# A graph-attention layer on one core: the order of the first 25 microseconds and of the last instructions

## The reference

```python
h = jnp.maximum(_layernorm(x, axis=-1), 0.0)
# the attention layer on h
h = node_features @ W.T + b_W
e = (h @ a1)[:, None] + (h @ a2)[None, :] + b_a[0]
e = jnp.where(e > 0, e, 0.2 * e)
scores = jnp.where(adjacency_matrix > 0, e, jnp.float32(NEG_INF))
attention = jax.nn.softmax(scores, axis=1)
h_prime = attention @ h
# and last
x = x + h_prime
```

## Time and profile before

| | |
|---|---|
| device time, median of 3 | 209.23 us (208.92 to 209.34) |
| the profiled execution | 209.82 us, its span 208.2 us |
| PE busy | 198.0 us, 95% of the span |
| DVE busy | 183.3 us, 88% |
| ACT busy | 141.4 us, 68% |
| POOL busy | 47.5 us, 23% |
| DMA | 75.66 MB, mean 363 GB/s |

### The profile page before, as it was taken

How to read it: one execution, slowest core, us unless ns; L and a number is a source line. 1 busy time by engine, 2 the same in 40 slices (tenths; PEclk the granted TensorE clock), 3 DMA queues, 4 the chain that set the end, 5 groups by cost and what they waited for, 6 DMA issues and landing times.

```text
span 208.2 us, 7164 instructions
## 1 busy us (share of the span) xinstructions
PE 198.0 (95%) x3176; PEld 191.8 (92%) x3176; DVE 183.3 (88%) x268; ACT 141.4 (68%) x129; POOL 47.5 (23%) x65
## 2 busy tenths in 40 slices
PE   0998999999999999999999999999999999999993
PEld 0686789899999999999999999999999999999992
DVE  3828997999999999987999998979998899989753
ACT  2388866997671777779775766798677737987000
POOL 1052879899950020440000000000000000000000
PEclk9999999999999999999999999999999999999999
DMA  5999999999999999999999999999999999980321
GB/s 180 352 416 406 404 402 410 404 404 404 413 422 405 409 408 408 405 411 408 406 407 408 390 391 416 409 407 408 410 407 406 378 416 409 411 336 37 104 66 40
DMA packets 24160, 75.66 MB, mean 363 GB/s; under 512 B 1600, under 2 KB 5952, under 8 KB 24000
## 3 DMA queue, kind: packets, MB, share of 16 engines
q1 hardware_dynamic: 23984, 75.06, 91.7%
q10 hardware_dynamic: 144, 0.13, 0.3%
HBM read 73.08 MB, written 2.11 MB: 361 GB/s over the span
## 4 chain that ended last, share of the span: by engine, by line
issue 60%; DMA 14%; PE 12%; ACT 5%; DVE 4%; POOL 3%; SPq 1%; POOLq 0%
DMA adj_sb<-in_adj_t 12%; ACT mask L380 5%; PE ps L752 3%; PE ps L762 3%; DMA wp<-in_w_pack 2%; DVE w L452 2%; PE ps L784 1%; PE ps L786 1%; PE ps L790 1%; SPq L313 1%; POOL tx L733 1%; POOL bad L738 1%; POOL tt L735 1%; POOL bad L737 1%; DVE stats L523 1%
## 5 line engine op out<-in xcount | busy, mean ns | idle before, releaser
L784 PE MATMUL ps<-V,w 128*128 128x129 f16 x1024 | 177.3, 219 | 0.7 <-DVE V L566 0.3
L786 PE MATMUL ps<-V,w 128*128 128x129 f16 x1024 | 177.3, 223 | 0.0
L790 PE MATMUL ps<-V,w 128*128 128x129 f16 x1024 | 177.3, 218 | 0.0
L380 ACT ACTIVATE mask<-adj_sb 128x2048 bf16<-128x2048 int32 x62 | 117.7, 1914 | 37.7 <-DMA adj_sb<-in_adj_t 31.5
L452 DVE SCALAR_TENSOR_TENSOR w<-g_row,pairs,mask 128x1024 f32<-128x1024 f32 x96 | 117.8, 1280 | 8.1 <-ACT mask L380 5.2
L790 PEld LDWEIGHTS ps<-V,w 128*128 128x128 f16 x1024 | 102.0, 100 | 0.0
L784 PEld LDWEIGHTS ps<-V,w 128*128 128x128 f16 x1024 | 99.2, 97 | 2.3 <-issue 1.2
L786 PEld LDWEIGHTS ps<-V,w 128*128 128x128 f16 x1024 | 99.8, 97 | 0.6 <-issue 0.6
L452 DVE SCALAR_TENSOR_TENSOR w<-ps,pairs,mask 128x1024 f32<-128x1024 f32 x32 | 38.7, 1275 | 0.4 <-issue 0.4
L742 POOL PARTITION_ALL_REDUCE bad<-bad x1 | 0.4, 380 | 114.7 <-DVE bad L505 114.7
L762 PEld LDWEIGHTS ps<-wp,hT 128*128 128x128 f32 x64 | 8.9, 209 | 2.0 <-issue 1.5
(11 more groups left out here) (87 smaller groups left out, 59.3 us busy)
## 6 DMA issues: line engine op xcount, KB each, us to landing
adj_sb<-in_adj_t SPq DMA_DIRECT2D x64, 1024.0 KB, 11.1
xT<-in_x_t SPq DMA_DIRECT2D x8, 256.0 KB, 7.5
x_sb<-in_x_p SPq DMA_DIRECT2D x3, 512.0 KB, 10.9
g_row<-g_dram SPq DMA_DIRECT2D x1, 1536.0 KB, 10.6
out<-xT SPq DMA_DIRECT2D x3, 512.0 KB, 11.8
x_sb<-in_x_p SPq DMA_DIRECT2D x2, 256.0 KB, 4.2
out<-xT SPq DMA_DIRECT2D x1, 192.0 KB, 2.1
out<-xT SPq DMA_DIRECT2D x3, 64.0 KB, 1.5
```

The lines of the kernel that those rows point to most:

```text
L380: nc.scalar.activation(mask[:, m % MASKS, :], adj_sb[:, m % HELD, :], ACT.Relu, scale=CONNECTED).then_inc(mask_ready, 1)
L784: nc.tensor.matmul(sums[:, bank, a, :], w16[:, m % SLOTS, col:col + P, 1], V[:, jt, 0:NF], start=(jt == 0 and a == 0), stop=False, skip_gr ...
L786: nc.tensor.matmul(sums[:, bank, a, :], w16[:, m % SLOTS, col:col + P, 1], V[:, jt, NF:2 * NF], start=False, stop=False, skip_group_check= ...
L790: last = nc.tensor.matmul(sums[:, bank, a, :], w16[:, m % SLOTS, col:col + P, 0], V[:, jt, 0:NF], start=False, stop=(jt == NT - 1), skip_g ...
```

## The change

Six pieces of order change, and eight products are added.

- PE: eight products of a matrix of ones with itself stand ahead of the wait for the first load, into a part of PSUM that is not read before it is written again. They wait only for POOL's memset of `ones`, which now comes first on POOL.
- SP: chunk 1 of the turned x is the second load instead of the fourth, chunk 2 stands ahead of x's third set.
- ACT: `relu_chunk(0)` and `relu_chunk(1)` stand ahead of both square roots; the table load for exponentials stands behind `take_chunk(1)` instead of ahead of `take_chunk(0)`.
- ACT: `relu_chunk(4)` stands behind `products(0)` and `highs(0)`, `weights(1)` behind `relu_chunk(5)`.
- DVE: `statistics(2)` is cut in two halves, of which one stands in the wait for the spread limit and one behind the shifts; `early_mask(0)` stands behind `pack(0)` and `scale_weights(0)`; `lows(0)` stands ahead of `weigh(0, 0)`; `scores(1)` stands between `weigh(0, 0)` and `weigh(0, 1)`; `statistics(3)` stands ahead of `weigh(1, 0)`.
- DVE: the last `rows` stands ahead of `check_sums`.

```diff
+    WARM = 8
...
                 load_xt(0)
+                load_xt(1)
                 load_x(0)
                 load_x(1)
-                load_xt(1)
+                load_xt(2)
                 load_x(2)
-                load_xt(2)
                 load_xt(3)
...
                     nc.scalar.activation(rstd[:, 0, 0:GI], mv[:, 0:GI, 1], ACT.Sqrt, bias=eps_col[:, 0:1]).then_inc(std_ready, 1)
-                    relu_chunk(0)
                     act.wait_ge(norm_ready, 1)
...
+                relu_chunk(0)
+                relu_chunk(1)
                 roots_part()
-                relu_chunk(1)
-                nc.scalar.activation(warm[:], zero_col[:], ACT.Exp)
                 take_chunk(0)
                 relu_chunk(2)
                 take_chunk(1)
+                nc.scalar.activation(warm[:], zero_col[:], ACT.Exp)
                 relu_chunk(3)
                 take_chunk(2)
                 weights(0)
                 take_chunk(3)
-                relu_chunk(4)
                 products(0)
                 highs(0)
-                weights(1)
+                relu_chunk(4)
                 take_chunk(4)
                 relu_chunk(5)
+                weights(1)
...
-                statistics(2)
                 scores(0)
...
+                statistics(2, 0, 4)
                 dve.wait_ge(t_spread, 1)
...
-                early_mask(0)
+                statistics(2, 4, 8)
                 pack(0)
                 scale_weights(0)
-                scores(1)
-                statistics(3)
+                early_mask(0)
+                lows(0)
                 dve.wait_ge(pairs_ready, 1)
                 dve.wait_ge(rows_spread, 2)
                 weigh(0, 0)
-                lows(0)
+                scores(1)
                 weigh(0, 1)
                 early_mask(1)
                 pack(1)
                 scale_weights(1)
+                statistics(3)
                 weigh(1, 0)
...
-                    if i == len(PIECES) - 1:
-                        check_sums()
                     rows(i)
+                check_sums()
...
+                nc.gpsimd.memset(ones[:], 1.0).then_inc(ones_set, 1)
...
-                nc.gpsimd.memset(ones[:], 1.0)
...
+                pe.wait_ge(ones_set, 1)
+                for _ in range(WARM):
+                    nc.tensor.matmul(ps[:, 7, 0:P], ones[:], ones[:], start=True, stop=True)
```

More of the change, by code:

```diff
@@ L171, in gat_layer_kernel @@
         constants_ready = sem("constants_ready")
+        ones_set = sem("ones_set")
         ident_ready = sem("ident_ready")
```

## The result

| | before | changed |
| --- | --- | --- |
| median of the runs, us | 209.07 (208.61 to 209.34, 4 runs) | 212.78 (211.83 to 213.63, 4 runs) |
| ratio, 95% interval | 1 | 1.0166 (1.0133 to 1.0200) |
| profiled execution, us | 209.82 | 213.63 |
| its span, us | 208.2 | 212.1 |
| mean granted clock | 1.0 | 0.988 |

The changed kernel is slower by 1.7%, about 3.5 us. The forecast was 209.1 with a range up to 210.6: wrong in size and in sign. The profile shows three losses: 2.0 us at the packing ahead of block 5, 1.5 us in the clock behind it, and 0.35 us at the end. The first scores came earlier, and nothing of that was left at block 5.

What follows compares the result with a forecast made beforehand. The prediction took PE's start of block 5, fed by DVE's `weigh` chain, and the end as bounds: 209.82 - 0.4 (start) + 0.3 (end) = 209.7 profiled, median 209.23 moved by -0.1 to 209.1; range 208.6 to 210.6 us.

Steps and rivals of the forecast that it cites:

- a shift of that second `weigh` goes through to 41.28 one to one: Block 1's second `weigh` on DVE, 26.83 to 28.10: any shift moves PE's start of block 5 at 41.28 equally.
- rival 2: `scores(2)` on DVE: POOL's late deviations become its bound, 0.8 us later than today, 210.3 us in all; chance 0.15.
- The 0.4 us at the second `weigh`: Block 1's second `weigh` would end at 27.65 instead of 28.10, and PE begin that half 0.4 us earlier.
- the new wait: DVE ahead of `lows(0)`: after its mask it idles some 0.8 us, with all its work queued behind.
- no mask runs in this stretch now: POOL's chain ahead of `scores(2)`: argument against another power of 3.03 us instead of some 1.7, which had overlapped DVE's mask.
- `scores(0)` near 12.5: First scores on DVE would begin at 12.45 instead of 14.25, 1.8 us gained.
- the norm as releaser of `centre_chunk(2)`: PE's centring of chunk 2 would wait last for the norm and begin at 9.85, today 11.66.
- no drain behind the table load: ACT's table load ahead of `weights(0)`: takes 1.28 us without the 1.38 us drain, which was given no chance.
- the end: DVE's last row ahead of the checks pushes the flag back: 0.3 us later, bounds 0 and 0.4.
- The limit at the end: The last `weigh` on DVE ends at 196.35 regardless of PE, so PE can be at most 0.5 us earlier.

Runs made afterwards that it cites:

- b_collide: Kernel before, with one more wait on POOL so its bias additions to the first two sets run beside DVE's packing of the third weights; 210.70 us, ratio 1.0060.
- b_stats3: Kernel before with one edit: `statistics(3)` behind `scale_weights(1)`, ahead of the `weigh` of block 1; 212.89 us, ratio 1.0189.
- after: The changed kernel as first measured and profiled, against the kernel before; 212.78 us, ratio 1.0166.
- after_again: The changed kernel measured again, with no edit, against the kernel before; 213.40 us, ratio 1.0175.
- a_tail: The changed kernel with `check_sums()` ahead of the last output row again, as before; 212.42 us, ratio 1.0137.
- a_stats3: The changed kernel with `statistics(3)` put behind `scores(1)`, ahead of the second `weigh` of block 0; 210.01 us, ratio 1.0036.
- best1: a_stats3 with the checks ahead of the last row again; 209.57 us, ratio 1.0020.
- best2: best1 with the loads in the order of the kernel before; 209.97 us, ratio 1.0036.
- a_small: The changed kernel with POOL's bias additions for sets 0 and 1 in eight pieces of 128x128 instead of two of 128x512; 211.88 us, ratio 1.0138.
- b_addb: The kernel before with POOL's bias additions for sets 0 and 1 moved behind all its halves; 209.12 us, ratio 1.0004.
- best3: best1 with POOL's bias additions for sets 0 and 1 behind all its halves; 208.78 us, ratio 0.9984; measured again 208.83 us, ratio 1.0008.

## Why the prediction was wrong

**The step that failed** is the first paragraph's "a shift of that second `weigh` goes through to 41.28 one to one". It took everything between 28.1 and 41.28 at the durations and waits of before; the stretch from the start of that `weigh` to block 5 grew from 14.45 to 17.11 us. In this pair of profiles the second `weigh` did come earlier, by 0.68 where 0.4 was forecast, but what follows it depends on where GpSimd stands, and the same change had moved the start of GpSimd's chain from 19.88 to 24.53. I followed GpSimd's chain to its deviations (rival 2) and stopped there; I did not follow it four instructions further, to the additions, and did not ask what they would lie beside. The collision cost 1.97 us in two clamps (b_collide: 1.48 from the same alone), the late release of `scores(2)` 0.54 and its held operation 0.16; b_stats3 has all of it from the one moved line.

**The 0.4 us at the second `weigh`** are not shown either, though the profile has 0.68. They were counted from a profile of before whose `weigh` (26.83) is the latest of four with that order (from 25.46 on); the changed order has 25.93 to 27.48. `scores(0)` does come earlier by about 1.4 us on the mean of these profiles, and the moved statistics and the new wait take all of it back, where the prediction let 0.4 through.

**Rival 2** had the right mechanism for half of it. It put the end of GpSimd's chain at 35.35, wanted at 35.5; measured 35.65, and ACT's copy was ready at 35.19. The difference lies in the main in one row, 0.80 at 25.53 against 0.24 at 32.97: GpSimd stood while DVE did `lows(1)` (25.55 to 26.23). The argument against it, "no mask runs in this stretch now", looked for one partner only. The row of 3.03 us in the earlier trace rows was the warning: it was read as a peculiarity of the power beside a mask. The rows fit a hold-up, since the power ended 0.04 us behind that mask (24.50 and 24.46), but no run was made to test this one.

**What the rows then showed of the hold-up.** In eight profiles with the long additions (after, after_again, a_tail, b_stats3, b_collide, a_stats3, best1, best2), every clamp that was held ended 0.04 us behind the end of the addition, whether it took 0.66 or 1.22 us in all (it does not run its own 0.18 behind it, as the theory of a_small had it), and a_small scales it with the length of the addition. The two additions take 2.51 to 2.54 us with the clamps beside them and without, so the one that holds loses nothing. The second operation of `scores(2)`, with two inputs, obeys the same: 36.71 in the changed kernel, where GpSimd's half ended at 36.67. In a_stats3 and the best versions the same operation began 0.01 to 0.03 us behind the start of a half and was not held, so a start this close does not decide it. The Trainium skill, "SBUF — State Buffer", Who interferes with whom, states it: DVE and GpSimd share a pair of ports as an exclusive lock, held for the whole instruction, wanted by DVE's `tensor_scalar` and cast in a two-port mode and, against a GpSimd instruction that reads SBUF, by its operations with two inputs in SBUF. The trace agrees in all three kinds, with the 1.13, 0.39 and 0.52 above; it does not show the mode or the ports. That rule spoke against the change and I did not weigh it.

**The clock behind the gap** was in no rival: 1.52 us in the profiled execution, none in the second, which was nearly as long (213.33 against 213.63) with a later start. Its share of the median is not known, and why the clock fell in one profile and not in the others stays open.

**Right:** `scores(0)` near 12.5 (11.94), the norm as releaser of `centre_chunk(2)` (forecast 9.85, measured 9.18; the load landed early enough to make the second statistics start at 7.16), the new wait ahead of `lows(0)` (0.88 against some 0.8), no drain behind the table load, and the end (0.3 forecast, 0.33 to 0.43 measured). Before, the last row ran inside the flag's wait for GpSimd's maximum, of which 0.29 us were left; now the whole 0.55 us are idle.

**The limit at the end** exists, but not at a fixed 196.35: the last `weigh` ended at 195.93, 195.94 and 196.37 in the three profiles in which PE took the last half block up 0.06 us behind it, and at 195.49 in b_addb, where PE was later. Against the 197.00 of before it lets PE be 0.6 to 1.0 us earlier, not a fixed 0.5; it is why best3, with block 5 1.4 us earlier than in the profile of before, ends only 1.0 us earlier.

## What to carry to other kernels

When an edit delays the work that feeds a side engine, follow that engine's whole queue and write down beside what each of its instructions will now run; an operation that was free where it stood may hold up another engine for its full length. A duration in a trace holds for its neighbours of that moment: where the same operation stands twice with different durations in the profile, find the partner before moving anything. And read the limits of both ends first: a start that gains 1.4 us is worth nothing if the moved work takes it back, and little when PE must wait for the last `weigh`. Last, a gain smaller than the spread of the start cannot be read from one profile of each kernel: compare a stretch that begins behind the start.

## What was not expected of the hardware

- DVE's two clamps, 0.18 us each, took up to 1.22 beside a GpSimd addition of 1.27 to 1.30 and then ended 0.04 us behind it; GpSimd's 0.24 us operation took 0.80 beside a DVE operation of 0.68 with two inputs, and ended 0.1 us behind it.
- After a gap of PE of 2.3 us the granted clock was at its lower level for part of the next 5 us in one profile (0.66 on the mean), and stayed at full in three other profiles with a gap of that kind (after_again, a_tail, b_stats3).
- With eight products of ones ahead of the first load, the first pair of 512 columns took 1.10 to 1.15 us in eight of twelve profiles, 1.35 to 1.72 in three and 2.06 in one; without them it took 2.05 or 2.06 in all six.
